# Two attention loops: both key tiles of a value product in one step, and the maxima's transposes ahead of the second row matmul

## What is computed

```python
scores = jnp.einsum('bhqd,bhkd->bhqk', q, k) * scale          # 16 heads, 256 x 512
scores = jnp.where(mask == 0, jnp.float32(-1e9), scores)      # first layer only
attn = jax.nn.softmax(scores, axis=-1)
x = jnp.einsum('bhqk,bhkd->bhqd', attn, v)
...
x = x + xattn0(layernorm(x), ctx, ctx, mask)
x = x + ffn0(layernorm(x))                                    # 16 experts, 4 of them, and a shared one
x = x + xattn1(layernorm(x), ctx, ctx)
x = x + ffn1(layernorm(x))                                    # 8 experts, 2 of them
```

## Time and profile before

| | us |
|---|---|
| median of 3 runs | 260.47 |
| lowest and highest | 258.6, 260.87 |
| profiled execution | 259.6 |
| its span | 257.8 |
| TensorE busy | 229.2 |
| VectorE busy | 186.8 |
| ScalarE busy | 155.5 |
| GpSimd busy | 77.8 |

### The profile page before, as it was taken

One profiled execution on the slowest core, in us unless ns is written; L12 is line 12 of the kernel. 1 busy time (PEld: TensorE's weight loads), 2 busy tenths in 40 slices (PEclk: granted clock), 3 DMA queues, 4 the chain that ended last, 5 costly groups with the idle time before them and its releaser, 6 DMA issues.

```text
span 257.8 us, 5097 instructions
## 1 busy us (share of the span) xinstructions
PE 229.2 (89%) x1656; PEld 136.4 (53%) x1656; DVE 186.8 (72%) x578; ACT 155.5 (60%) x225; POOL 77.8 (30%) x223
## 2 busy tenths in 40 slices
PE   2879899999999999999899779999988989989871
PEld 1553444445444547868676444454444447767660
DVE  7678786776676384677755897888865657789864
ACT  6675896666964762341232467777775674696570
POOL 4581442465522100100200241444422042344321
PEclk9999999999999999999999999999999999999997
DMA  6768799920110038700033492400000000000000
GB/s 204 255 203 167 195 154 165 320 79 18 47 61 3 3 66 154 148 2 0 0 113 73 130 356 80 112 4 0 4 0 3 0 0 4 1 0 3 0 20 22
DMA packets 18180, 20.41 MB, mean 79 GB/s; under 512 B 1553, under 2 KB 15609, under 8 KB 17825
## 3 DMA queue, kind: packets, MB, share of 16 engines
q1 hardware_dynamic: 17578, 19.16, 29.4%
q10 hardware_dynamic: 576, 0.94, 1.2%
HBM read 15.90 MB, written 4.19 MB: 78 GB/s over the span
## 4 chain that ended last, share of the span: by engine, by line
PE 58%; DVE 22%; issue 8%; DMA 4%; ACT 3%; POOL 2%; SPq 1%; DVEq 1%; POOLq 0%; ACTq 0%
PE bank L372 11%; PE bank L447 9%; PE bank L425 8%; PE bank L421 5%; DVE st L1056 4%; PE bank L545 4%; PE bank L565 4%; PE bank L546 3%; DVE row_max L871 3%; PE bank L620 2%; PE bank L378 2%; ACT q_stack L1364 2%; DVE shared_area L1094 1%; DMA aw<-in_attn_w 1%; DMA k_bounce<-early 1%
## 5 line engine op out<-in xcount | busy, mean ns | idle before, releaser
L1379 ACT ACTIVATE probs<-bank 128x1024 f32<-128x1024 f32 x64 | 64.3, 1023 | 14.1 <-PE bank L425 9.0
L868 DVE CUSTOM_DVE_ANT_0 discard<-bank,bias_q 128x512 bf16<-128x512 f32 x64 | 43.3, 690 | 17.5 <-PE bank L372 16.1
L372 PE MATMUL bank<-k_stack,q_stack 72*128 72x512 bf16 x128 | 48.4, 384 | 4.5 <-DVE row_max L871 1.8
L871 DVE TENSOR_REDUCE row_max<-bank 128x1 f32<-128x512 f32 x64 | 42.0, 687 | 9.4 <-PE bank L372 5.8
L425 PE MATMUL bank<-q_stack,k_stack 102*128 102x256 bf16 x256 | 43.7, 272 | 0.2 <-ACT q_stack L1364 0.2
L447 PE MATMUL bank<-probs,v_ext 128*32 128x256 f32 x512 | 40.3, 391 | 0.2 <-ACT o_sb L1386 0.2
L1364 ACT COPY q_stack<-bank 6x512 bf16<-6x512 bf16 x32 | 18.5, 578 | 27.7 <-PE bank L394 27.6
L425 PEld LDWEIGHTS bank<-q_stack,k_stack 102*128 102x128 bf16 x256 | 24.8, 98 | 17.1 <-issue 1.4
L1620 POOL CAST max_part<-row_max 128x4 bf16<-128x4 f32 x32 | 6.3, 195 | 81.3 <-DVE row_max L871 45.2
L372 PEld LDWEIGHTS bank<-k_stack,q_stack 72*128 72x128 bf16 x128 | 12.2, 96 | 27.8 <-issue 12.6
L421 PE MATMUL bank<-bias_k,idb 128*128 128x512 bf16 x64 | 24.3, 380 | 0.3 <-ACT q_stack L1364 0.2
(11 more groups left out here) (187 smaller groups left out, 360.4 us busy)
## 6 DMA issues: line engine op xcount, KB each, us to landing
k_stack<-k_bounce SPq DMA_DIRECT2D x9, 384.0 KB
q_bounce<-q_part SPq DMA_DIRECT2D x12, 192.0 KB, 2.9
k_bounce<-early SPq DMA_DIRECT2D x4, 384.0 KB, 3.3
experts_w<-in_wu SPq DMA_DIRECT2D x1, 1024.0 KB, 4.9
early<-in_wu SPq DMA_DIRECT2D x1, 1024.0 KB, 7.1
experts_w<-in_wg SPq DMA_DIRECT2D x1, 816.0 KB, 14.1
experts_w<-in_wu SPq DMA_DIRECT2D x1, 816.0 KB, 16.4
experts_w<-in_wd SPq DMA_DIRECT2D x1, 768.0 KB, 16.9
```

What stands on the lines that cost most here:

```text
L372: mm(bank[:, qt, :], q_stack[0:STACK, b, h, qt * 128:(qt + 1) * 128], k_stack[0:STACK, b, h, :], start=True, stop=True).then_inc(for_max, 1)
L868: ins = dve.tensor_tensor_reduce(discard[:, qt, :], bank[:, qt, :], bias_q[:, qt, :], 1.0, LOWEST, ALU.add, ALU.max, o)
L871: ins = dve.tensor_reduce(o, bank[:, qt, :], AX.X, ALU.max)
L1379: act.activation(probs[:, n % (2 * HG), :], bank[:, at:at + 2, :].rearrange("p a n -> p (a n)"), ACT.Exp, scale=SCALE).then_inc(exp_done, 1)
```

## The change

Both edits are in TensorE's part of the loop and hold for both layers. In odd steps the transposes of the maxima stand behind the column matmuls and ahead of the second row matmul, no longer behind it (the early steps in which the transposes already stood ahead of the columns stay as they are). Values are computed in odd steps alone, two key tiles one after the other: the tile of the step itself and that of the next, even step. The output's transposes stay in the even steps, and nothing changes in the programs of the other engines.

```diff
                     if columns:
                         score_cols(m, range(0, KT // 2))
                         score_cols(m, range(KT // 2, KT))
+                    if transposes and not at_once:
+                        max_transpose(l * HEADS // MG + (s - 3) // MG)
                     if rows and not (transposes and at_once):
                         score_rows(n, 1)
                     if l == 0 and s < FIRST_LAGS[0]:
                         keep_busy(5, 2)
-                    if transposes and not at_once:
-                        max_transpose(l * HEADS // MG + (s - 3) // MG)
                     if s % HG == (PV_LAG + 1) % HG and s >= PV_LAG + HG:
                         o_transpose(l * B * NG + (s - PV_LAG) // HG - 1)
-                    if s >= PV_LAG:
-                        values(l * B * NG + (s - PV_LAG) // HG, (s - PV_LAG) % HG)
+                    if s >= PV_LAG and (s - PV_LAG) % 2 == 0:
+                        for kt in ((s - PV_LAG) % HG, (s - PV_LAG) % HG + 1):
+                            values(l * B * NG + (s - PV_LAG) // HG, kt)
```

## The result

| | before | after |
|---|---|---|
| median (20 runs each) | 259.12 us | 260.68 us |
| lowest and highest | 258.19, 260.87 | 259.67, 262.0 |
| ratio after/before, 95% interval | | 1.005 (1.0029 to 1.007) |
| profiled execution, its span | 259.6, 257.8 | 260.22, 258.4 |

The change costs half a per cent. Behind this near-zero stand two movements of nearly 2 and nearly 3 us, of opposite signs. Four marks in TensorE's timeline make them visible: the first row matmul (L372), the transpose of the combine weights (L493), with which the first loop is over, T of step 3 of the second loop, and the end of the span. The same marks are read in all later kernels.

What follows compares the result with a forecast made beforehand. TensorE bounds both loops, with hardly any room on other engines in the second; first loop -1.9, second +2.7, together +0.8 us: profiled 259.6 becomes 260.4, median 261.3, range 257.6 to 263.9 (8 in 10).

Steps and rivals of the forecast that it cites:

- pair with a divide, second loop: Second loop, two steps with VectorE's divide: the maxima's transposes wait for it, 3.88 us against 3.42 before.
- pair without one: Second loop, two steps without a divide: values wait for ScalarE's exponential and output copy, 3.30 us against 3.20 before.
- T not before the even R1 + 1.78: Steps 15, 19, ...: maxima's transposes cannot start until 1.78 us after the even step's second row matmul starts.
- second loop, steps 13 to 27: Second loop's body: four pairs with a divide lose 0.46 each, three without lose 0.10 each, +2.1 us.
- second loop's end: Second loop's end: two values calls of step 33 delay the gate's matmuls and the routing chain, +0.4 us (0 to +0.9).
- first loop, four steps: First loop's body: four steps take 8.18 us against 8.38, a gain of 0.20.
- first loop, steps 11 to 27: First loop's body: the gain per four steps, held four times, -0.8 us.
- first loop to step 11: First loop's start: earlier maxima's transposes keep 0.2, paired values of steps 9 and 10 add 0.2, -0.4 us (0 to -0.5).
- first loop's end: First loop, steps 27 to 40: six merged pairs win 1.4 us, less waits at steps 31, 33 and 37, -0.7 (-1.4 to 0).
- The rival in which the divide does not hold T: Both loops: the divide finishes sooner, so waits of 0.23 and 0.64 us vanish, 258.1 us; chance 0.12.
- the one in which the switches are saved in full: Both loops: 30 pairs each save 0.23 us of tiling switches, -6.9 us, to 253.6; chance 0.05.
- ScalarE's exponential does not start later than reckoned: Rival: even step's exponential starts 0.3 us later than 0.64 after column matmuls, delaying values, +3.0, 264.3 us; chance 0.17.

Runs made afterwards that it cites:

- the two matmuls added: Kernel with only the second loop changed, plus one keep-busy TensorE matmul in each of that loop's steps 6 and 7: 262.45 us, ratio 1.012.
- the short divide: Changed kernel with the divide's reciprocal left out and its product replaced by a copy: 257.64 us, ratio 0.9944.
- the other pair of kernels: First loop paired, maxima's transposes after second row matmul behind a divide; second loop unpaired, transposes ahead: 255.59 us; plus keep-busy matmuls in second-loop steps 6 and 7: 255.96.

## Why the prediction was right

260.4 was forecast for the profiled execution and 260.22 measured, 261.3 for the median and 260.68 measured. Both come so near in part by luck. The span grew by 0.60, but without the 0.34 by which the first row matmul happened to come sooner it is 0.94, against 0.8 forecast. And the median was built on that of three executions, 260.47; the median of 20 is 259.12, and from there the sum would have given 259.9, with 260.68 measured. The account stands on the steps, all but the third read at V, a mark that the edits don't move:

| step of the prediction | forecast | measured | read from |
|---|---|---|---|
| pair with a divide, second loop | 3.88 | 3.88 | V to V, 160.72 to 164.60 |
| pair without one | 3.30 | 3.30 | V to V, 164.60 to 167.90 |
| T not before the even R1 + 1.78 | 1.78 | 1.79 | 162.39 to 164.18 |
| second loop, steps 13 to 27 | +2.1 | +2.03 | V to V, 23.37, now 25.40 |
| second loop's start | +0.2 | +0.12 | first T to V of step 13, 17.90, now 18.02 |
| second loop's end | +0.4 | +0.54 | V of step 27 to the end of the span, 71.74, now 72.28 |
| first loop, four steps | 8.18 | 8.17 | V 46.73 to 54.90 |
| first loop, steps 11 to 27 | -0.8 | -0.76 | V to V, 33.59, now 32.83 |
| first loop to step 11 | -0.4 | -0.48 | first row matmul to V, 19.43, now 18.95 |
| first loop's end | -0.7 | -0.49 | V of step 27 to L493, 25.39, now 24.90 |

The period of the second loop grew by 0.52 (6.65 to 7.17) where 0.56 was forecast, because the prediction's sum of rounded starts gave 6.62 for the kernel before.

**The body.** The saving of 0.23 for each V that follows a V was a real one: in the kernel after, a V of 16 instructions holds the engine for 1.01 to the next row matmul, 0.44 more than one of 8, where a lone call costs 0.66. The Trainium skill (TensorEngine Tiling (Array Packing), Key Properties) says that a change of tiling mode drains the engine; the trace agrees in that a change costs this time. That it is the change of tile and not of data type is seen where only the tile changes: from V to L471, a float32 matmul of full width, it takes the same 0.57 (189.88 to 190.45 with the transposes alone). The saving was paid out in the first loop, where the other engines have room. In the second it was spent on waits whose size followed from latencies that stood in the trace of before: matmul to maximum, divide to hand-back of bank 7 (0.76 was read once, and it is 0.76 here, from D at 163.42 to T at 164.18), and in the pair without a divide the exponential and copy ahead of V. The refill of R0's bank, worked out to 0.3 of waiting, is there with 0.3, but sets no pair's length by itself: it alone would have V at 167.87 in the kernel after, the copy has it at 167.90. The experiments moved each cause by itself: T back behind R1 gave 0.22 per four steps, the reciprocal left out 0.24 (7.17 to 6.93), a maximum 0.27 shorter gave 0.28 in the one pair and nothing in the other. The rival in which the divide does not hold T is refuted by these, and the one in which the switches are saved in full by the four steps of 7.17. ScalarE's exponential does not start later than reckoned either: the pair it limits measured 3.30, as reckoned with the 0.64.

**The loop ends were estimated, and there a reason was wrong and a term missing.** The start of the first loop gave 0.48 where 0.4 was forecast, but not from the two sources named. I had put 0.2 of it to the merge of steps 9 and 10; at V of step 11 the values alone give nothing, and the transposes alone give all of it. T of step 5 came 7.66 us behind the first row matmul in place of 8.63 (27.27 - 19.61 and the earlier trace rows). In TensorE's timeline of the kernel before, T stood behind an R1 that itself waited 0.58 for its bank:

```profile
28.36 0.39 PE L372 MATMUL bank<-k_stack,q_stack 72*128 72x512 bf16 x1 [0.58 <-DVE row_max L868]
```

T's move takes it out from behind a stalled instruction, so T comes 0.97 sooner and not 0.22. Little of this is kept: the next column matmuls start 0.34 sooner (9.58 behind the first row matmul, now 9.24, at 28.85), since ahead of them R0 waits for the row maximum in its bank, and at V of step 9 it is 0.23 (15.09, now 14.86), the prediction's 0.2. The other 0.25, between V of step 9 and V of step 11, has the size given to the merge, but it comes with the transposes alone too (15.09 to 19.43 before, 14.85 to 18.94). What the same move gives at the end of a loop where nothing is paired (bank 7 earlier for L464 and L471) I had not listed at all. In the kernel after it adds nothing, as seen above.

The end of the first loop gave 0.49 where 0.7 was forecast. The waits were named rightly and sized too small, 0.7 in sum against these 1.55 in TensorE's timeline of the kernel after:

```profile
80.74 0.27 PE L394 MATMUL bank<-idb,max_part 128*128 128x128 bf16 x2 [0.47 <-DVEq L886]
...
84.94 1.07 PE L447 MATMUL bank<-probs,v_ext 128*32 128x256 f32 x16 [0.48 <-ACT o_sb L1387]
...
91.99 1.07 PE L447 MATMUL bank<-probs,v_ext 128*32 128x256 f32 x16 [0.60 <-ACT o_sb L1387]
```

These are T of step 31 (0.3 forecast) and V of steps 33 and 37 (0.2 each). With the row matmuls gone, a step is shorter, and the copy of the output, which stands behind an exponential of 1.02 that it can't pass, is all the later against V. Against them stands a term that the prediction put at nothing: four waits of 0.23 of the kernel before in that stretch (at L464, L471, L340 and L481) are gone, 0.92 in sum. Six merged pairs give 1.4; with 1.55 lost and 0.92 won back that makes 0.75, and 0.26 of it I can't place. One more small wait stands in the body: in step 27 a column matmul waits 0.27 for `probs`.

```profile
70.10 0.38 PE L421 MATMUL bank<-bias_k,idb 128*128 128x512 bf16 x1 [0.27 <-ACT probs L1380]
```

**The medians** differ by 1.56 us, more than the 0.60 of the spans. Of this the transfer at the start explains 0.34 for the pair of profiles shown. The fall of the clock, taken up in the last section, does not explain the rest: 4 of the 20 executions of the kernel after have one and 13 of the 79 of the kernel before beside the experiments, about as many, and the medians of those without are 260.51 and 259.01. The rest stays open; the profiled execution of the kernel before is one of the slower ones (259.6 against a median of 259.12), that of the kernel after one of the faster.

## What to carry to other kernels

A switch saved on the busiest engine pays only where its neighbours have slack: lay out a period of the loop with every hand-back of a buffer as a chain of latencies (here maximum, divide, hand-back: 1.78 us), and see how much of the moved work was covering it. Two loops with the same code can have opposite signs, so try an edit per loop; here the gain of one (-1.7) was hidden behind the loss of the other (+2.7), and keeping only what pays gave -3.6 us. When an instruction is moved out from behind another, look for the stall of the one it stood behind and for the buffer that it frees earlier, not only for a duration; here the move was worth 0.9 us in each loop where nothing was paired. Read such a gain at a mark that the edit does not move: at T itself, 0.22 of it is only T's new place.

## What was not expected of the hardware

In some executions TensorE's granted clock falls. In four of the profiled ones it did so in the second loop behind step 7. The stretch from 152 to 158 us, first of the kernel with the second loop alone changed, same columns as above:

```profile
152.00:158.00 6.00, 5.92 (x36) 3.01 (x37) 3.14 (x8) 2.73 (x5) 2.29 (x9) 0.72 0.38 104
```

of its repetition:

```profile
152.00:158.00 6.00, 5.90 (x27) 2.63 (x31) 3.72 (x8) 2.68 (x4) 1.62 (x6) 0.51 0.50 140
```

and with the two matmuls added:

```profile
152.00:158.00 6.00, 5.54 (x44) 3.07 (x44) 4.35 (x10) 4.09 (x6) 2.30 (x9) 1.00 0.40 112
```

A granted clock of 0.51 is the lower of the two levels, 1.2 in place of 2.4 GHz, for nearly the whole stretch, and 0.72 is a mixture of both. Ahead of it TensorE works with gaps, as its timeline in the kernel with the second loop alone changed shows:

```profile
150.89 0.39 PE L372 MATMUL bank<-k_stack,q_stack 72*128 72x512 bf16 x1 [0.31 <-DVE row_max L876]
...
152.08 0.60 PE L372 MATMUL bank<-k_stack,q_stack 72*128 72x512 bf16 x1 [0.21 <-DVE row_max L876]
...
153.07 1.49 PE L378 MATMUL bank<-early,idb 128*128 128x512 bf16 x3
```

The three matmuls of L378 take 1.49, at the full clock 0.81 (at 153.00 in the kernel with the two added matmuls). The price is 1.3 to 2.7 us of the trace. These four executions (the transposes alone, the second loop alone twice, the short divide) have an overall clock of 0.983 to 0.991. So has the profiled one with the pairs in even steps (0.990), whose clock falls elsewhere: 0.72 from 10 to 16 us, and its first row matmul comes at 21.60. The other profiled ones, the kernel after's among them, have 0.993 or more. An overall clock at or below 0.991 thus tells a fall, but not its place. Of the executions of before beside the experiments 13 of 79 had one, with a median of 260.86 against 259.01. It was 16 of 102 in kernels whose second loop has T behind R1 (before, the values alone, the first loop alone), 29 of 86 in those with T ahead there for most steps, among them 8 of 10 where only the second loop was changed, and 2 of 12 with the two matmuls. So an edit can cost more than its steps lose (+4.9 and +4.0 were measured where they lose 2.7) by making the fall more frequent. That gaps ahead of step 8 are the cause fits the added matmuls (1 of 6 against 8 of 10 for the same kernel), but on so few runs, and it does not fit the other pair of kernels, with 1 of 6 without the two matmuls and 1 of 6 with them; and the kernel before, which shows it seldom, has gaps there too (TensorE busy 4.93 of 6 us from 146 to 152). What decides it stays open.
